# ScalarE copies the idle ends of a bitonic merge's groups twice a merge instead of at every stage, both halves of the keys in one copy

## What is computed

```
def _L0_conv_ref(x):
    B, H, W, F = x.shape
    M = H * W
    x3 = x.reshape(B, M, F)
    corr = jnp.einsum('bmf,bnf->bmn', x3, x3) / F
    s = -jnp.sort(-corr, axis=-1)
    ranks = jnp.round(jnp.linspace(1.0, M - 1, NB_POOLS)).astype(jnp.int32)
    pooled = jnp.take(s, ranks, axis=-1)
    return pooled.reshape(B, H, W, NB_POOLS)
...
x = x + _L0_conv_ref(_ln_c(x))
t = t + _L0_ffn_ref(_ln_t(t), ...)
```

## Time and profile before

| what | value |
|---|---|
| time, median of 3 runs | 31163.97 us (31161.8 to 31172.99) |
| span of the profiled execution | 31832.6 us |
| VectorE busy | 28357.2 us (89%) |
| TensorE matmul busy | 25816.8 us (81%) |
| ScalarE busy | 22199.6 us (70%) |
| GpSimd busy | 15519.9 us (49%) |

### The profile page before, as it was taken

The page is one execution under the profiler, slowest core; times in us unless marked ns, Lnnn a source line. Parts: engine busy times, 40 slices in busy tenths (PEclk is TensorE's granted clock), DMA queues, the critical chain, the costliest instruction groups (busy, mean ns, idle before and its releaser), DMA issues. The chain is left out here.

```text
span 31832.6 us, 519908 instructions
## 1 busy us (share of the span) xinstructions
PE 25816.8 (81%) x174835; PEld 11754.5 (37%) x175348; DVE 28357.2 (89%) x30738; ACT 22199.6 (70%) x34415; POOL 15519.9 (49%) x9076
## 2 busy tenths in 40 slices
PE   3888888888888888888888888888888888883474
PEld 3555533333333333333333333333333333332464
DVE  6888859999999999999999999989999999997435
ACT  1777777777777777777777777767777777774730
POOL 0000018888888888888888888887000000001510
PEclk8999999999999999999999999999999999996655
DMA  2000000000000000000000000000000000000103
GB/s 89 2 2 2 2 18 5 6 7 7 6 7 6 13 7 7 7 7 7 6 12 6 7 7 7 6 6 6 12 6 6 6 6 6 6 6 12 15 12 131
DMA packets 651302, 393.71 MB, mean 12 GB/s; under 512 B 425132, under 2 KB 604336, under 8 KB 646448
## 3 DMA queue, kind: packets, MB, share of 16 engines
q1 hardware_dynamic: 338034, 311.42, 3.1%
q0 software_dynamic: 290304, 22.40, 1.1%
q10 hardware_dynamic: 20288, 25.70, 0.2%
HBM read 196.49 MB, written 162.34 MB: 11 GB/s over the span
## 5 line engine op out<-in xcount | busy, mean ns | idle before, releaser
L1399 ACT ACTIVATE z<-psum 128x1024 f32<-128x1024 f32 x14208 | 14105.4, 1026 | 4046.7 <-PE psum L1157 2696.9
L1503 POOL DMA_INDIRECT sorted_d<-word_s,place_s x8192 | 14683.9, 1792 | 2643.7 <-issue 2476.9
L1157 PE MATMUL psum<-z,net 64*64 64x512 f32 x103424 | 13548.6, 619 | 2790.8 <-ACT z L1399 2536.0
L1357 DVE TENSOR_TENSOR arena<-arena 128x1536 f32<-128x1536 f32 (+17 forms) x6016 | 11654.5, 1937 | 1170.1 <-ACT arena L1438 637.6
L1358 DVE TENSOR_TENSOR arena<-arena 128x1536 f32<-128x1536 f32 (+17 forms) x6016 | 11647.7, 1936 | 0.0
L1157 PEld LDWEIGHTS psum<-z,net 64*64 64x64 f32 x103424 | 3128.9, 132 | 12044.9 <-issue 12018.0
L1673 POOL DMA_INDIRECT arena<-table_d,arena x752 | 762.1, 1013 | 7506.8 <-DVE arena L1597 7284.2
L1438 ACT ACTIVATE arena<-arena 128x2048 f32<-128x2048 f32 (+15 forms) x5248 | 3149.0, 600 | 466.9 <-DVE arena L1358 466.6
L978 ACT ACTIVATE arena<-cst,arena 128x128 bf16<-128x128 f32 x8320 | 2633.6, 389 | 608.9 <-PE psum L906 514.3
L1497 POOL DMA_DIRECT2D word_s<-words_d x64 | 37.6, 588 | 4798.8 <-issue 4663.0
L1164 PE MATMUL psum<-z,net 64*128 64x512 f32 x8192 | 1901.0, 601 | 208.4 <-ACT z L1399 199.9
(11 more groups left out here) (217 smaller groups left out, 18338.8 us busy)
## 6 DMA issues: line engine op xcount, KB each, us to landing
sorted_d<-word_s,place_s POOLq DMA_INDIRECT x8192
y_d<-ys SPq DMA_DIRECT2D x256, 256.0 KB
arena<-y_d SPq DMA_DIRECT2D x64, 1024.0 KB, 5.6
arena<-in_x SPq DMA_DIRECT2D x34, 512.0 KB, 5.1
x<-in_x SPq DMA_DIRECT2D x65, 256.0 KB
xnt_d<-arena SPq DMA_DIRECT2D x32, 512.0 KB, 3.1
hk_d<-arena SPq DMA_DIRECT2D x32, 512.0 KB, 4.3
arena<-hk_d SPq DMA_DIRECT2D x4, 4096.0 KB, 14.1
```

The lines of the kernel that those rows point to most:

```text
L1157: last = nc.tensor.matmul(psum[n * HALF:(n + 1) * HALF, 2 * s + r, :], b.net[rr, at:at + HALF], flat[rr, n * BANK:(n + 1) * BANK], start=T ...
L1357: nc.vector.tensor_tensor(hi_out, hi_in, lo_in, ALU.max)
L1399: last = nc.scalar.activation(flat, bank, ACT.Abs)
L1503: pool.indirect_dma_start(out=b.sorted_d[:, :], out_offset=bass.IndirectOffsetOnAxis(ap=place_s[:, s, j:j + 1], axis=0), in_=word_s[:, s, ...
```

## The change

Only the ends that a later stage reads in the wrong buffer are copied. In a merge by p the full stage (p, p) writes everything. The stages then alternate between two buffers, and what stage (p, p) left in its own target stays there unharmed until a stage with a smaller k reads it. In the other buffer two pieces are missing: the part from p/4 to p/2 at either end of a group (`which` = 0), read by stage k = p/4, and the outermost p/8 (`which` = 1), read from stage k = p/16 on. `edges_of` picks these blocks. ScalarE issues the first copy at stage k = p/2 and the second at k = p/4, each behind the first half of that stage's ticks, and each for both rows at once; both wait only for stage (p, p). That makes 10 copies a pair. VectorE waits for them at k = p/4 and at k = p/16.

The keys of both rows now stand in one range, and VectorE's two turns of a stage are the two halves (h) of it. While the lower 1024 keys are apart, the range of the higher ones is 6144 long, g = 0 before g = 1, and the lower ones are behind it. At (1024, 1024) `bring_together` reads the blocks of one row from where they are and writes the row to its final place. At three stages, `FIRST_MERGE`, (1024, 1024) and (1024, 512), a half needs both halves of the stage before (`across`).

```
-N_CARRIED = sum(k < p for p, k in STAGES[:N_FULL])
+MERGES = sorted({p for p, _ in STAGES})
+N_CARRIED = 2 * len(MERGES)
...
+def edges_of(buf, p, which):
+    w, at, apart = ((p // 4, 1, 5), (p // 8, 0, 15))[which]
+    return buf.rearrange("p (n m w) -> p n m w", m=2 * p // w, w=w)[:, :, at::apart, :]
+
+def carried_before(s):
+    p, k = STAGES[s]
+    return 2 * MERGES.index(p) + (k <= p // 4) + (k <= p // 16)
...
+            def block_of(buf, n, g):
+                n_high = (M - LO) // 1024
+                at = n * 1024 + g * (M - LO) if n < n_high else 2 * (M - LO) + (n - n_high) * 1024 + g * LO
+                return buf[:, at:at + 1024]
+
+            def bring_together(source, target, g):
+                for n in range(0, M // 1024, 2):
+                    hi_in, lo_in = block_of(source, n, g), block_of(source, n + 1, g)
+                    at = g * M + n * 1024
+                    nc.vector.tensor_tensor(target[:, at:at + 1024], hi_in, lo_in, ALU.max)
+                    last = nc.vector.tensor_tensor(target[:, at + 1024:at + 2048], hi_in, lo_in, ALU.min)
+                return last
...
-                        if s > 0 or after_first:
-                            dve.wait_ge(sorted_[g], i * N_FULL + s)
-                            dve.wait_ge(carried[g], i * N_CARRIED + kept_before(s))
-                        for source, from_, to in sources(s, g):
-                            hi_in, lo_in = compared(source[:, from_:to], p, k)
-                            hi_out, lo_out = compared(half[s % 2][g][:, from_:to], p, k)
-                            nc.vector.tensor_tensor(hi_out, hi_in, lo_in, ALU.max)
-                            last = nc.vector.tensor_tensor(lo_out, hi_in, lo_in, ALU.min)
-                        last.then_inc(sorted_[g], 1)
+                        elif s > 0:
+                            across = (p, k) in ((1024, 1024), (1024, 512)) or s == FIRST_MERGE
+                            dve.wait_ge(sorted_, (i * N_FULL + s) * 2 + (0 if across else h - 1))
+                            if h == 0 and k in (p // 4, p // 16):
+                                dve.wait_ge(carried, i * N_CARRIED + carried_before(s))
+                        if s == 0:
+                            last = compare(fresh[:, here], target[:, here], p, k)
+                        elif s == FIRST_MERGE and h == 1:
+                            old, new = slice(here.start, edge), slice(edge, 2 * M)
+                            compare(source[:, old], target[:, old], p, k)
+                            last = compare(fresh[:, new], target[:, new], p, k)
+                        elif (p, k) == (1024, 1024):
+                            last = bring_together(source, target, h)
+                        else:
+                            last = compare(source[:, here], target[:, here], p, k)
+                        last.then_inc(sorted_, 1)
...
-            def carry(i, s, g):
-                p, k = STAGES[s]
-                act.wait_ge(sorted_[g], i * N_FULL + s)
-                act.wait_ge(carried[g], i * N_CARRIED + kept_before(s))
+            def carry(i, p, which):
+                s = first_of(p)
+                act.wait_ge(sorted_, (i * N_FULL + (s + 1)) * 2)
...
-                    for g in range(2):
-                        if k < p and s < N_FULL:
-                            carry(i, s, g)
-                        middle = len(ticks) // 2
-                        for tick in (ticks[middle:] if g else ticks[:middle]):
+                    middle = len(ticks) // 2
+                    for tick in ticks[:middle]:
+                    ...
+                    for which in range(2):
+                        if k == p >> (which + 1):
+                            carry(i, p, which)
+                    for tick in ticks[middle:]:
```

More of the change, by code:

```diff
@@ L285, in compared, with first_of @@
     return m[:, :, :, 0, :], m[:, :, :, 1, :]
[L288 to L296, removed]
+def first_of(p):
+    return STAGES.index((p, p))
+def edges_of(buf, p, which):
[4 more added lines that the diff above has]
+    return 2 * MERGES.index(p) + (k <= p // 4) + (k <= p // 16)
 RANKS = [int(r) for r in np.round(np.linspace(1.0, M - 1, D))]
@@ L1011, in pool_rows @@
     sem, carve, psum, sb = b.sem, b.carve, b.psum, b.sb
-    half = [[b.arena[:, (2 * n + g) * M:(2 * n + g + 1) * M] for g in range(2)] for n in range(2)]
-    fresh = [b.arena[:, (4 + g) * M:(5 + g) * M] for g in range(2)]
-    fresh_v = b.arena[:, 4 * M:6 * M].rearrange("p (g m) -> p g m", g=2)
+    keys = [b.arena[:, 2 * n * M:2 * (n + 1) * M] for n in range(2)]
+    fresh = b.arena[:, 4 * M:6 * M]
+    fresh_low = fresh[:, 2 * (M - LO):].rearrange("p (g m) -> p g m", g=2)
+    fresh_high = fresh[:, 0:2 * (M - LO)].rearrange("p (g m) -> p g m", g=2)
     both = [b.arena[:, 2 * n * M:2 * (n + 1) * M].rearrange("p (g m) -> p g m", g=2) for n in range(2)]
@@ L1037, in pool_rows @@
     fe_copied = [sem(f"fe_copied{s}") for s in range(SLOTS)]
-    sorted_ = [sem(f"sorted{g}") for g in range(2)]
-    carried = [sem(f"carried{g}") for g in range(2)]
+    sorted_, carried = sem("sorted"), sem("carried")
     tailed = sem("tailed")
@@ L1327, in sparse, with compare @@
                 last.then_inc(tailed, 1)
[L1329 to L1336, removed]
+            def compare(source, target, p, k):
+                hi_in, lo_in = compared(source, p, k)
+                hi_out, lo_out = compared(target, p, k)
+                nc.vector.tensor_tensor(hi_out, hi_in, lo_in, ALU.max)
+                return nc.vector.tensor_tensor(lo_out, hi_in, lo_in, ALU.min)
+            def block_of(buf, n, g):
[9 more added lines that the diff above has]
+                return last
             def sort(i, after_first):
+                edge = 2 * (M - LO)
                 for s, (p, k) in enumerate(STAGES):
@@ L1342, in sort @@
                         continue
-                    for g in range(2):
-                        if s == 0 and g == 0:
+                    source, target = keys[(s - 1) % 2], keys[s % 2]
+                    whole = edge if s < FIRST_MERGE else 2 * M
+                    for h in range(2):
+                        here = slice(h * whole // 2, (h + 1) * whole // 2)
+                        if s == 0 and h == 0:
                             for n in range(SLOTS):
                                 dve.wait_ge(fe_copied[n], (i + 1) * PER_PAIR)
-                        if s == 0 and after_first:
-                            dve.wait_ge(tailed, i * SPARSE)
-                        if s > 0 or after_first:
-                            dve.wait_ge(sorted_[g], i * N_FULL + s)
-                            dve.wait_ge(carried[g], i * N_CARRIED + kept_before(s))
-                        for source, from_, to in sources(s, g):
-                            hi_in, lo_in = compared(source[:, from_:to], p, k)
-                            hi_out, lo_out = compared(half[s % 2][g][:, from_:to], p, k)
-                            nc.vector.tensor_tensor(hi_out, hi_in, lo_in, ALU.max)
-                            last = nc.vector.tensor_tensor(lo_out, hi_in, lo_in, ALU.min)
-                        last.then_inc(sorted_[g], 1)
@@ new lines, in sort @@
+                            if after_first:
+                                dve.wait_ge(tailed, i * SPARSE)
+                        elif s > 0:
[13 more added lines that the diff above has]
+                            last = compare(source[:, here], target[:, here], p, k)
@@ L1390, in front @@
                         if tick + 1 == len(FRONT[0]) and s == 0 and not (isinstance(i, int) and i == 0):
-                            for g in range(2):
-                                act.wait_ge(sorted_[g], (i - 1) * N_FULL + FRESH_READ)
+                            act.wait_ge(sorted_, ((i - 1) * N_FULL + FRESH_READ) * 2)
                         at = (j * SLOTS + s) * UNIT_GROUPS * WIRES
-                        last = nc.scalar.activation(fresh_v[:, :, at:at + UNIT_GROUPS * WIRES], bank, ACT.Copy,
+                        to, at = (fresh_low, at) if at < LO else (fresh_high, at - LO)
+                        last = nc.scalar.activation(to[:, :, at:at + UNIT_GROUPS * WIRES], bank, ACT.Copy,
                                                     bias=-1.0)
@@ L1456, in period @@
                     ticks = ticks_of(s)
-                    for g in range(2):
-                        if k < p and s < N_FULL:
-                            carry(i, s, g)
-                        middle = len(ticks) // 2
-                        for tick in (ticks[middle:] if g else ticks[:middle]):
[L1462 to L1465, removed]
+                    middle = len(ticks) // 2
+                    for tick in ticks[:middle]:
+                        if has_next:
+                            front(i + 1, tick)
+                        if has_last:
+                            ffn_piece(i - 1, tick)
+                    for which in range(2):
```

(7 more changed lines are left out.)

9 lines of the change are left out of this document (5 added, 4 removed).

## The result

The changed kernel takes 31044.76 us, the median of five runs (31026.07 to 31060.7), against 31163.97 of five (31160.42 to 31172.99): 119 us less, a ratio of 0.996 with a 95% interval of 0.9948 to 0.9973. The forecast was 341 us less. The direction was right and the time lies in the range, near the upper end; the gain is a third of what was forecast.

The account below looks back on a forecast made before the run. ScalarE with TensorE was taken to bound the kernel by a little, VectorE nearly. Gains of 4.7 us (late) to 8.7 (early) a period, taken as 5.5, times 62 gave 341 us off 31164: 30823 us, range 30550 to 31120.

Parts of the forecast that it names:

- What bounds the kernel: Late periods: ScalarE with TensorE bound it by a little, 374.1 us a period; VectorE's sort nearly, 368.1.
- forecast floor 369.6: VectorE's sort in the changed kernel: 368.1 us a period, plus 0.7 for the loop and 0.8 added work.
- What a copy costs the ticks' chain: ScalarE's activations after TensorE: each copy hides 0.59 us in a tick's gap; only its remaining length counts.
- 35.0 us a pair: ScalarE's copies: busy time removed, from 49.2 us a pair to 14.2, most of it hidden before.
- 8.7 us: All merges of a period: saving on ScalarE's chain of ticks, from 374.1 us to 365.4.
- What waits remain: Stage 19, p = 512: copy begins at t = 136.1, VectorE waits 2.3 us; late period 371.9 us, 4.7 less.
- 136.8 I started from: Stage 18, kernel before: start of ScalarE's copy of 2048 within a period, read from the first profile's timeline.
- The choice between the stretches: All 62 periods: a gain of 5.5 us each, between late 4.7 and early 8.7, 341 us in all.
- What it adds on VectorE: Stages (1024, 1024), 8 and three waits for the instruction right before: 0.8 us a pair more.
- That all waits go: Rival: VectorE never waits for a copy; 30370 to 30730 us, middle 30550. Chance 0.18.
- The Trainium skill's fixed cost: ScalarE instructions between SBUF operands: 224 cycles each; by it 35.0 us would count in full, ticks' chain 339 us.
- That the copies come too late: Rival: late copies at stages 10, 19, 29 and 40, some 3.5 us each; 31635 us. Chance 0.08.

Follow-up runs that it names:

- experiment 7: Changed kernel plus 14 unused ScalarE copies of 440 elements a pair, two at each of stages 10 to 16; 31260.28 us, ratio 1.0023.
- experiment 1: The kernel before, run and profiled again with no edit; 31176.38 us, profiled span 31174.7 us.
- experiment 6: Changed kernel with the first copy of the p = 256 merge one tick later; 30924.85 us, ratio 0.9917.
- Experiment 4: Changed kernel with the first copy of every merge one tick earlier; 31037.43 us, ratio 0.9954.
- experiment 5: Kernel before with copies twice a merge, each row by itself where its copies stood, 20 a pair, rows apart on VectorE; 30743.42 us, ratio 0.9858.
- 10: Changed kernel with first copies moved: p = 256 one tick later, p = 512 two earlier, p = 1024 and p = 2048 one earlier; 30799.57 us, ratio 0.988.
- experiment 9: Kernel before with 20 one-row copies a pair, both rows' copies standing where the changed kernel's joined copy stands; 30889.91 us, ratio 0.9909.

## Why the prediction fell short, step by step

**What bounds the kernel** was right. In a normal execution too VectorE waits 6.4 us a period and ScalarE 2.7, and without copies the period is 369.4 (forecast floor 369.6).

**What a copy costs the ticks' chain** was right: 0.59 us of each hide in a tick, by the earlier trace rows, and experiment 7 found 0.5 us for 1.1. The 35.0 us a pair of ScalarE's time were a sum of durations that overlap; its busy time fell by 24. The 8.7 us do not rest on that.

**What waits remain** is the step that failed, at the sentence "From there to the p = 512 merge it saves 1.1 + 1.9 = 3.0 us". I had tied ScalarE to VectorE at stage 1 and let it run free from there. It is tied again at stage 9, where its copy of p = 256 needs all of VectorE's stage 8. In the kernel before, in experiment 1's profile (stage 0 at 27610.01), the tick behind the second row's copy starts at t = 60.2:

```profile
27610.01 1.76 DVE L1357 TENSOR_TENSOR arena<-arena 128x1536 f32<-128x1536 f32 x1 [2.38 <-ACT z L1399]
```

```profile
27668.39 1.91 ACT L1438 ACTIVATE arena<-arena 128x2048 f32<-128x2048 f32 x1 [0.26 <-DVE arena L1358]
27670.20 1.92 ACT L1399 ACTIVATE z<-psum 128x1024 f32<-128x1024 f32 x2
```

In the changed kernel the same tick starts at 27534.22, t = 60.3, and the copy ahead of it has waited 0.81 us. All that ScalarE had saved before that place (the 1.1 us of p = 128, and one whole copy of p = 256) is gone here. In the mean of all periods the tick starts at 60.3, against 60.8 in the kernel before. Behind it only small copies were left to save, 0.6 us by the prediction's own prices.

The second part is TensorE's clock, which the prediction put at nothing. While ScalarE waits for VectorE, TensorE has no free slot and stands idle. In the period shown it had been idle for 2.54 us before its next matmul (upper row, changed kernel). Eight matmuls of a slot then took 1.98 us; in experiment 1, at the same place, they took 1.09 us (lower row).

```profile
27535.37 1.98 PE L1165 MATMUL psum<-z,net 64*64 64x512 f32 x8 [2.54 <-ACT z L1429]
...
27671.35 1.09 PE L1157 MATMUL psum<-z,net 64*64 64x512 f32 x8 [1.99 <-ACT z L1399]
```

The granted clock of the changed kernel's trace, in stretches of 2 us, fell there from full speed (1.00, 2.4 GHz) to its lower level (0.50, 1.2 GHz) and was back before 27540. It is the number behind POOL's:

```profile
27532.00:27534.00 2.00, 0.83 (x8) 0.00 (x0) 1.82 (x9) 1.60 (x1) 0.00 (x0) 1.00 0.00 0
27534.00:27536.00 2.00, 0.63 (x4) 0.33 (x8) 2.00 (x3) 2.00 (x3) 0.00 (x0) 0.78 0.00 0
27536.00:27538.00 2.00, 2.00 (x12) 0.71 (x4) 2.00 (x3) 0.73 (x2) 0.00 (x0) 0.50 0.00 0
27538.00:27540.00 2.00, 2.00 (x12) 0.62 (x11) 2.00 (x2) 0.86 (x2) 0.00 (x0) 0.87 0.00 0
```

So ScalarE's next tick came 3.19 us after this one, where experiment 1 has 2.30. In 28 of the 59 periods between 5400 and 27500 us the clock was at the lower level for a while between t = 55 and 85, and in those the copy at stage 18 began at 138.8 in the mean; in the 31 others at 136.9. In the kernel before it was there in 14 of 58 periods, in experiment 6 in none of 59.

Together: the copy at stage 18 began at 138.4 in the period shown and at 137.8 in the mean, not at 136.1. The mean wait was 4.3 us, not 2.3: 2.0 x 62 = 124 us of the missing 222. Of the lateness of 1.7 us the clock is 0.9 (28/59 of 1.9) and the tie the rest. The tie took more than that rest, as the 136.8 I started from stands in the profile of the earlier trace rows; experiment 1 has 136.0 in the mean, so that with the tick's 2.3 us only 0.5 of the 3.0 us were left. Experiment 6 bears out both: with the copy of stage 9 a tick later the one of stage 18 begins at 135.8, 2.0 us earlier than in the changed kernel, 0.9 by the clock and 1.1 by the tie, where 1.3 was expected. Experiment 4 fits, with a gain of 81 us lost, but it moved the copies of stages 1, 28 and 39 too. That TensorE's idle time brings the clock down is read from the order of events in the rows; no run changed it alone.

**The choice between the stretches** is the second. I took 5.5 us a period between 4.7 (late) and 8.7 (early). The early stretch was that of an unusual execution (experiment 1), so that 4.7 was the term: 0.8 x 62 = 50 us. The rest is 48 us. The spans of the two normal profiles differ by 132 us, of which the 62 periods, 2.5 us each, make 154; other parts of the program go 22 the other way, 13 of them ahead of the first pair's end (5041.23 against 5028.48). Why is not settled; the five runs of the changed kernel alone spread over 35 us.

**What it adds on VectorE**, 0.8 us, was too much. The sort without ticks went from 368.1 to 368.3. That is two things: the joined layout costs 0.6 us (368.3 against 367.7 in experiment 5), and 0.4 come back (367.7 against 368.1), which I had not counted; what differs there on VectorE's queue is fewer waits for `carried`. A wait for the instruction right before costs 0.1 us rather than 0.18: the gap at stage (1024, 1024) is in these rows, 2.31 us from start to start where 2.20 is usual.

```profile
28416.58 2.28 DVE L1339 TENSOR_TENSOR arena<-arena 128x2044 f32<-128x2044 f32 x1
28418.78 2.28 DVE L1340 TENSOR_TENSOR arena<-arena 128x2044 f32<-128x2044 f32 x1
28421.09 1.23 DVE L1353 TENSOR_TENSOR arena<-arena 128x1024 f32<-128x1024 f32 x1
```

**The rivals.** That all waits go (0.18) didn't happen with this order, but it does with another (experiments 5 and 10). The Trainium skill's fixed cost for each ScalarE instruction ("VectorE: DVE Perf Modes", § The TRN2 errata) is no bound here, as said: the kernel with 20 copies beats that with 10. That the copies come too late (0.08) was the right mechanism at one of its four places; it cost 4.3 us, below the 6.4 at which it would have decided.

**What joining the rows costs.** The changed kernel is 301 us behind experiment 5. Place: 146 us (9 against 5). Length and layout: 155 us (the changed kernel against 9), 2.5 us a period, of which the layout is 0.6. Both are good to some 20 us. The remaining 1.9 is near what two lengths of 0.85 us make (a joined copy takes 1.90 us, one of a row 1.05): the joined copy is longer by that at stage 18, and at stage 9 all of it comes after VectorE's second half, where of two row copies only one does. That split of the 1.9 is argued, not shown; the clock is in it too, at its lower level between t = 55 and 85 in about half the periods of both kernels (28 of 59, and 32 of 58 in experiment 9).

## What to carry to other kernels

Where two engines hand work to each other through queues in program order, a saving counts only up to the next place at which one waits for the other; go through every such place in turn before the savings are added up. Then the place of an instruction in its queue can matter more than its length: here 24 us of ScalarE's busy time a period gave 2.5 us, and a copy moved by one tick 1.3 to 1.9. A wait of the engine that empties TensorE's slots can cost more than its own length: here TensorE's clock fell behind it, and the next tick took 3.19 us for 2.30. Joining two copies saves a fixed cost but makes the first reader wait for both halves.

## What was unexpected of the hardware

The profiled execution of the kernel before took 31832.6 us where the timed ones took 31160 to 31213. Its mean granted clock was 0.942, where the timed runs of the same kernel have 0.950 or 0.951. From 5400 to 27500 us TensorE was at the lower level for 10.2 us a period, against 3.8 in experiment 1. The 6.4 us more, at half speed, could cost 3.2 us of work at most (an estimate from these numbers), half of the 6.6 us by which the early periods were longer; and the changed kernel has 10.7 us of it with periods of 373.8. So the clock can be a part but not the whole, and it may as well have followed from the waits. Its early periods were 383.1 us long against 376.3, and ScalarE had waits of up to 3.2 us there for something outside the core, of which the normal profile lists none in the same stretch. What it was is open. Where the span of a trace doesn't fit the timed runs, as here, it pays to look for the stretch that does: its late periods, 376.6 us, were like those of experiment 1.
